# Attention: fourteen loaded pieces of the next stack divided 3, 4, 3 and 4 over four gaps instead of 5, 2, 5 and 2

## The reference

```
energy = einsum('bhqd,bhkd->bhqk', q, k)        # 4 batches, 16 heads, 1024 x 1024
att    = softmax(energy, axis=-1) / D ** 0.5
out    = einsum('bhqk,bhkd->bhqd', att, v)
```

## Time and profile before

| what | value |
|---|---|
| median of three runs | 1863.22 us |
| the profiled execution's own time | 1859.63 us |
| span of the profile, first to last instruction | 1857.5 us |
| PE, busy share of the span | 97% |
| GpSimd (POOL), busy share of the span | 66% |
| VectorE (DVE), busy share | 68% |
| ScalarE (ACT), busy share | 45% |
| q1, SP's queue of DMAs | 200.10 MB, 35.3% of 16 DMA engines |
| q0, GpSimd's queue (the accumulates) | 66.11 MB, 17.5% of 16 DMA engines |

### The profile page before, as it was taken

One profiled execution on the slowest core, in us unless ns is written; L12 is line 12 of the kernel. 1 busy time (PEld: TensorE's weight loads), 2 busy tenths in 40 slices (PEclk: granted clock), 3 DMA queues, 4 the chain that ended last, 5 costly groups with the idle time before them and its releaser, 6 DMA issues. The chain is left out here.

```text
span 1857.5 us, 27080 instructions
## 1 busy us (share of the span) xinstructions
PE 1810.5 (97%) x9510; PEld 1211.9 (65%) x9510; DVE 1254.3 (68%) x1986; ACT 834.5 (45%) x1545; POOL 1217.6 (66%) x679
## 2 busy tenths in 40 slices
PE   8989999999999999999899999999999999999997
PEld 4678888888888788888555545555555555554376
DVE  4655655655645575665877777777777777777288
ACT  3213123123123122222366666666666666666465
POOL 2665465465465242342488888888888888898665
PEclk9999999999999999999999999999999999999899
DMA  7410100100103657685777787878777877775796
GB/s 269 121 35 23 57 34 23 56 34 23 56 1 114 209 181 247 211 256 205 193 157 184 179 180 176 186 176 185 176 184 175 187 179 180 181 162 123 211 386 267
DMA packets 135373, 287.10 MB, mean 155 GB/s; under 512 B 23984, under 2 KB 41520, under 8 KB 127200
## 3 DMA queue, kind: packets, MB, share of 16 engines
q1 hardware_dynamic: 102996, 200.10, 35.3%
q0 software_dynamic: 9264, 66.11, 17.5%
q10 hardware_dynamic: 23008, 19.54, 3.3%
HBM read 134.68 MB, written 84.19 MB: 118 GB/s over the span
## 5 line engine op out<-in xcount | busy, mean ns | idle before, releaser
L1619 DVE TENSOR_REDUCE at_mrow<-banks 128x1 f32<-128x512 f32 x976 | 594.2, 681 | 162.5 <-PE banks L1465 162.4
L1715 POOL TENSOR_TENSOR at_sums<-at_probs 128x2048 f32<-128x2048 f32 x127 | 596.7, 4698 | 88.3 <-DMA at_sums<-at_sums 70.8
L1599 ACT ACTIVATE at_probs<-banks 128x512 f32<-128x512 f32 x1024 | 518.4, 624 | 179.9 <-PE banks L1483 174.9
L1465 PE MATMUL banks<-early_ks,early_qs 96*128 96x512 f32 x976 | 406.3, 416 | 8.4 <-DVE at_mrow L1619 4.6
L1483 PE MATMUL banks<-early_qs,early_ks 98*128 98x512 f32 x1024 | 409.4, 418 | 1.8 <-ACT at_probs L1599 1.8
L1465 PEld LDWEIGHTS banks<-early_ks,early_qs 96*128 96x128 f32 x976 | 184.7, 189 | 138.7 <-DVE at_mrow L1619 85.8
L1483 PEld LDWEIGHTS banks<-early_qs,early_ks 98*128 98x128 f32 x1024 | 193.7, 190 | 108.7 <-ACT at_probs L1599 84.5
L1495 PE MATMUL banks<-at_probs,at_v 128*32 128x512 f32 x2048 | 252.5, 611 | 1.7 <-DMA at_v<-v_scratch 1.7
L66 PE MATMUL banks<-l_nt,l_weights 128*128 128x512 f32 x768 | 179.2, 394 | 5.4 <-DVEq L1193 4.3
L657 ACT ACTIVATE l_gt<-banks,mod 128x512 f32<-128x512 f32 x60 | 45.1, 777 | 300.2 <-PE banks L526 263.9
L66 PE MATMUL banks<-l_ht,l_weights 128*128 128x512 f32 x768 | 177.4, 390 | 1.9 <-issue 1.9
(11 more groups left out here) (147 smaller groups left out, 2155.2 us busy)
## 6 DMA issues: line engine op xcount, KB each, us to landing
at_sums<-at_sums POOLq DMA_DIRECT2D x63, 1024.0 KB, 8.0
qk_scratch<-qk_out SPq DMA_DIRECT2D x64, 512.0 KB, 6.0
early_ks<-qk_scratch SPq DMA_DIRECT2D x48, 512.0 KB, 4.9
early_qs<-qk_scratch SPq DMA_DIRECT2D x96, 256.0 KB, 5.5
attn_scratch<-at_out SPq DMA_DIRECT2D x32, 512.0 KB, 7.3
o_a<-attn_scratch SPq DMA_DIRECT2D x32, 512.0 KB, 12.7
chunk_in<-x SPq DMA_DIRECT2D x8, 1024.0 KB, 5.4
v_scratch<-qk_v ACTq DMA_DIRECT2D x32, 256.0 KB, 3.1
```

The lines of the kernel that those rows point to most:

```text
L1465: pe.matmul(em[n % 3][:], qs[0:96, slot, half, j, c * P:(c + 1) * P], ks[0:96, slot, j, keys * CH:(keys + 1) * CH], start=True, stop=True) ...
L1599: nc.scalar.activation(probs[:, i % 4, j, :], et[n % 3][:], ACT.Exp).then_inc(exp_done, 1)
L1619: nc.vector.tensor_reduce(mrow[:, half, keys, u:u + 1], em[n % 3][:], AX.X, ALU.max).then_inc(max_done, 1)
L1715: nc.gpsimd.tensor_tensor(into, probs[:, a], probs[:, a + 1], ALU.add).then_inc(pair_ready, 1)
```

## The change

Only `load_part` changes. The DMAs are the same ones, with the same sizes, semaphores and order of queues; some are issued in another part.

```diff
-                    load_stack_keys(sp, sh, ks, g, slot, (0, 1))
+                    load_stack_keys(sp, sh, ks, g, slot, (0,))
                     load_stack_queries(sp, sh, qs, g, slot, 0, (0,))
                 if part == 1:
+                    load_stack_keys(sp, sh, ks, g, slot, (1,))
+                    load_stack_queries(sp, sh, qs, g, slot, 0, (1, 2))
+                if part == 2:
                     load_stack_keys(sp, sh, ks, g, slot, (2,))
-                if part == 2:
-                    load_stack_queries(sp, sh, qs, g, slot, 0, (1, 2))
-                    load_stack_queries(sp, sh, qs, g, slot, 1)
+                    load_stack_queries(sp, sh, qs, g, slot, 1, (0,))
                 if part == 3:
+                    load_stack_queries(sp, sh, qs, g, slot, 1, (1, 2))
                     load_v(g, slot)
```

## The result

The changed kernel takes 1905.43 us (median of 6 runs) against 1863.61 us for the kernel before beside it: a ratio of 1.0223, with a 95% interval of 1.021 to 1.0236. It is slower by 42 us. The forecast was slower, with 1872 us and an upper end of 1896; the rival "the whole backlog goes first" had been priced at 1902.

The account below looks back on a forecast made before the run. GpSimd's chain of accumulates and additions was taken to bound attention. Gains of 0.87 us and losses of 1.2 us, each twice a group, gave 0.66 us times 13, 8.6 us more: 1872 us, range 1852 to 1896.

Parts of the forecast that it names:

- the whole backlog goes first: Rival: all added loads precede accumulates behind parts 1 and 3; 1902 us; 17% together with the other costly case.
- The chain that sets the time: Attention, groups 1 to 13: GpSimd's accumulates and second additions alternate in a closed chain, 52.92 us a group.
- the floor of 52.15: Group 14's time without stack loads, 52.15 us; the stage could gain at most 0.77 us a group.
- The heavy gaps: Issue to next second addition behind parts 0 and 2: five units to three, 8.97 to 8.1 us.
- no gain at all: Bound for accumulates behind parts 0 and 2: they stay at 8.97 us, since 8.8 was seen without a load.
- The light gaps: Issue to next second addition behind parts 1 and 3: two units to four, 7.73 to 8.9 us; bounds 7.73 and 10.1.
- The lower bound: Behind parts 1 and 3, 7.73 us if all added loads are served behind the accumulate, at no cost.
- The sum: Attention: 2 x (8.1 + 8.93) + 19.52 = 53.58 us a group against 52.92, 8.6 us more over 13 groups.
- The faster one: Rival: an accumulate waits only for the load in service; 52.1 us a group, 1853 us; 25% chance.
- the turn-taking rule: Each DMA engine takes turns between its queues, a packet of descriptors at a time; by it 1853 us would be forecast.
- a case that did not come: Accumulates behind parts 0 and 2 are not relieved, the others lose 1.2 us twice a group: 1894 us; shares the 17%.
- What cost nothing: SP's moved issues add no wait; v lands with 5.4 us to spare before PE's wait for the stack.

Follow-up runs that it names:

- d43_split: Loads divided 4, 3, 4, 3 instead of the 5, 2, 5, 2 before; in parts 1 and 3 two units issued at the landing, one behind the widening: 1848.81 us.
- relief_only: Changed kernel with the four query DMAs added to parts 1 and 3 left out from group 3's stack on: 1847.22 us.
- half_p1: Changed kernel with part 3's two added queries kept in part 2, so only part 1 is heavier (units 3, 4, 5, 2): 1886.69 us.
- half_p3: Only part 3 made heavier, units 5, 2, 3, 4 against 5, 2, 5, 2 in the kernel before: 1885.94 us.
- d70: All stack loads issued at the landing in parts 0 and 2, units 7, 0, 7, 0 against 5, 2, 5, 2 in the kernel before: 1922.61 us.

## Why the prediction was wrong

**The chain that sets the time: right.** With GpSimd's accumulates as the clock of groups 1 to 13, the loss is there and nowhere else, and PE's wait for the accumulate grew as was said. Freed of it, a group takes 52.0 to 52.1 us (`d43_split`, `relief_only`), just under the floor of 52.15 that group 14 gave.

**The heavy gaps: right in size, in part by luck.** The sum counts from an issue to the next second addition. Behind parts 0 and 2 this was 8.21 and 8.08 us, and 8.1 had been taken. But the 8.1 was the mean of two landings, and these accumulates landed in 7.63 and 7.52. What made up the difference is mostly the wait for ScalarE behind the stretches at 1.2 GHz, which the prediction did not have. The bound of "no gain at all" did not come true: after the change 18 of the 26 accumulates behind parts 0 and 2 landed in 7.1 to 7.2 us. The 8.8 us of group 14 was the exception, which recurs (`relief_only` has landings behind parts 0 and 2 of up to 9.3 us); why is open.

**The light gaps: the step that failed.** The prediction said: "I take one of the two added units as ahead and one as behind", 8.9 us. Measured were 10.40 and 10.07 to the next addition, and 10.26 and 9.80 to the landing: the upper bound of 10.1. The working from the queue's rate (0.52 MB at 0.22 MB/us, 2.4 us) was good; the choice between the bounds was not. What stood behind it, that the last load goes out only shortly before the accumulate, is no reason to count it as behind: in group 1 after the change 0.07 us of head was enough. `half_p1`, `half_p3` and `d70` say the same of other parts and other head starts. The lower bound was wrong as well. It put a load that is served behind the accumulate at nothing, and the accumulate of group 7 with all its loads behind it landed in 9.64 us.

**The sum: right but for that term.** With the measured times to the next addition, 8.15 and 10.24 on average, it gives 2 x (8.15 + 10.24) + 19.52 = 56.3 us a group, and 56.28 were measured. The light gaps alone, 10.24 instead of 8.93, are 2.6 of the 2.7 us a group by which the forecast fell short, 34 of 35 us. The start of 8.97 and 7.73 was read from one group, where the means of 13 are 8.79 and 7.90; that mattered little. Of the cost by way of PE's clock, 11 us, the prediction said nothing. It is inside the measured 8.15 and 10.24.

**The rivals.** The faster one, by which only the load in service goes ahead, is out, and with it the use that the prediction made of the turn-taking rule: the output stage's rows don't carry over to an accumulate behind several loads. The queues did share the engines where the loads went out behind the accumulate (group 7 above), and even there it landed late. The second rival is what happened. It had 17% together with a case that did not come; the earlier trace rows, where a store waited for all of what came first, should have counted for more than the output stage.

**What cost nothing.** This held: SP's moved issues added no wait, and PE waited for v's landing once, for 0.4 us. Only PE's wait for the placed maxima grew a little, from 1.3 to 3.8 us in the matmuls.

## What to carry to other kernels

When transfers of two queues meet, ask what is still queued when the important one is issued, and price all of it as ahead: bytes over the measured rate, less the head start. A transfer issued just behind the important one costs as well. Dividing loads evenly over gaps is no aim in itself; each gap holds as many bytes as it can finish before its critical transfer, and a gap entered late holds fewer. Where a late transfer makes the tensor engine stand still, look at its granted clock behind the wait: the wait may not be the whole cost.

## What the runs showed of the hardware

Behind parts 1 and 3 of the changed kernel an accumulate of 1 MB waited for nearly all that SP had issued earlier, up to three DMAs (1 MB) and also one issued 0.07 us before it: where all three were ahead, at most 0.2 MB of them moved after its first packet. In the other direction it depends on the distance. A store issued 2.2 us behind an accumulate moved nothing while q0 had the engines; loads issued 0.55 to 1.5 us behind one moved beside it, and it landed in 9.64 us. With nothing ahead the first packet of an accumulate moved 1.43 to 1.47 us after its issue, and it landed in 6.9 to 7.2 us in most cases; single ones took 8.4 to 9.2 us with nothing of SP's queue moving at all (`d70`, behind parts 1 and 3). The runs do not say why.
